# First-level diagonal blocks laid out by ScalarE in free score columns, and fifth-level blocks written without a masked copy, in a two-layer kernel

## The chip, the cores and the metric

The kernel runs on one core of a Trainium2 chip. The metric is the device time in microseconds of one launch; the median of the runs counts. Engines are TensorE (PE in the profile; PEld is its weight load), VectorE (DVE), ScalarE (ACT), GpSimd (POOL) and SyncE (SP), which only issues DMAs here. All run their own instruction streams and meet in semaphores that are written out by hand.

## The reference

Input x is 4 x 1024 x 256 in float32. Two layers follow each other, each an attention-like block and a feed-forward block with modulated layer norms. The change touches one place, the complex linear recurrence of the second layer's first block:

```
c = (silu(x @ W_in.T + b_in) @ W_qkva.T + b_qkva)   # complex q, k, v, a; 8 heads of 32
a = a * (rsqrt(mag2) * sigmoid(log(mag2)))
h_t = a_t * h_(t-1) + k_t (outer) v_t                # associative scan along the sequence
y = einsum('blhd,blhde->blhe', q, h)                 # then W_y, silu, W_out
```

The other parts are a delta-rule attention, a gated mixture of 16 small experts, and a mixture of 8 large experts.

## The kernel before, in words

The sequence is cut into 8 segments of 128 positions, all 4 batches at once. A function `turn` is emitted once per segment on each engine; in it the second part of one segment (`rest`) is interleaved with the delta rule of the next (`nxt`) and the projections of the one after (`pre`). After the segments the large experts run.

In a segment the recurrence is evaluated as masked products of queries and keys, in levels. `HG = 2` groups of `HP = 4` heads alternate. Level k = 0 is the diagonal. Levels k = 1 to 5 (`INNER = 5`) pair neighbours inside blocks of `BLK = 32` positions: at level k the queries of the odd runs of m = 2^(k-1) positions meet the keys of the even runs before them. Levels 6 and 7 join blocks of 32 and of 64. Between two levels VectorE multiplies decay factors into the queries and keys (the loop over `lev` and `hg`, L1454 to L1471 on VectorE; `lev` = k - 1), and TensorE's `level(hg, k)` (L2113) computes the raw scores of level k into PSUM banks 4 hg to 4 hg + 3.

Where the scores go, for one head group:

- `nears[hg]` holds the 32 x 32 diagonal blocks, 4 heads x 4 batches x 2 (real and imaginary) x 32 columns a partition; for group 0 it lies in the tile `h_tok`, for group 1 in `arena`. GpSimd zeroes it and the full score tile `score` earlier in the segment (signal `zeroed`, counts 1 to 6).
- k = 0: VectorE's masked copy at L1362 takes the diagonal from PSUM.
- k = 1: VectorE takes the scores from PSUM by four masked copies, one for each block of 32 partitions (L1370), writing every second column of the near tile. They signal `masked`.
- k = 2 to 5: ScalarE's `take_blocks` (L881) copies the block diagonals from PSUM into `raws[hg]` in four pieces (signal `block_ok`), and VectorE makes one masked copy of 128 partitions from there into the near tile (L1379, signal `masked`).
- Then ScalarE's `lay_near` (L834) lays the near tile into the full scores, `lay_middle` (L845) and `lay_far` (L854) add levels 6 and 7 from PSUM; TensorE's `outputs` (L2128, L2133) follows.

Masks are in `near_masks`. The order on every engine is the order of the code. On VectorE each step of the loop is: the products, a wait for `scored` of the level that still reads the queries, the new queries and keys (signals `q_ready`, `k_ready`), the masked copy of the next level, and a wait for its end. TensorE's `level` waits for the keys, the queries, and for the signal that the former scores have left its banks: `masked` at k = 1 and 2, `block_ok` at k = 3 to 6. ScalarE waits, in front of its first `take_blocks`, for the sixth `q_ready` and the second `k_ready`, since `raws` lies in a table that level 1 reads. SyncE issues the load of the next x behind the first `k_ready`.

Of the kernel before, what the change touches and what calls it, by code (L numbers as in the profile page):

```python
# [24 lines left out]
ACT = mybir.ActivationFunctionType  # L25
AX = mybir.AxisListType

P = 128
B, L, D = 4, 1024, 256
KC = D // P  # L30
SEG = 128
# [91 lines left out]
def build(nc, ins, out):  # L123
    with ExitStack() as ctx:
# [132 lines left out]
        def level_table(hg, lev):  # L257
            n = NT >> lev
            if lev == LEVELS:
# [14 lines left out]
                 for v in (h_tok[:, :, :].rearrange("p b d -> p (b d)"), y2_flat[:, 2 * NT:4 * NT])]  # L274
        Hx, o = carve(o, [P, B, 2, HP, 2 * HD1])
# [85 lines left out]
        masked = signal("masked", rest=12)  # L361
        block_ok = signal("block_ok", rest=8)
# [299 lines left out]
        def _(act):  # L662
# [11 lines left out]
            def turn(seg, rest, nxt, pre):  # L674
                def at(s, k):
                    return s.handle, s.base(seg) + k
# [107 lines left out]
                if rest:  # L784
# [43 lines left out]
                    def lay_near(hg):  # L828

                        act.wait_ge(*at(masked, 2 * INNER + hg + 1))  # L830
                        for pair in range(2):
                            for n in range(NCH):
                                blk = slice(BLK * n, BLK * n + BLK)
                                ins_ = act.activation(score_pairs[hg][pair][blk, :, :, :, blk].rearrange("p h b r t -> p (h b r) t"),  # L834
                                                      nears[hg][blk, 2 * pair:2 * pair + 2].rearrange("p h b r t -> p (h b r) t"),
                                                      ACT.Copy)
                        ins_.then_inc(*up(laid, me))
# [35 lines left out]
                    def take_blocks(k, hg):  # L873
# [5 lines left out]
                        for n in range(NCH):  # L879
                            blk = slice(BLK * n, BLK * n + BLK)  # L880
                            ins_ = act.activation(  # L881
                                raws[hg][blk].rearrange("p (h g t) -> p h g t", h=HP, t=half),
                                banks_[blk, 4 * hg:4 * hg + HP, :].rearrange("p h (g c) -> p h g c", g=2 * B)
                                [:, :, :, half * n:half * n + half], ACT.Copy)
# [4 lines left out]
                    act.wait_ge(*at(q_ready, 3 * HG))  # L889
                    act.wait_ge(*at(k_ready, HG))  # L890
                    for k, hg in itertools.product(range(2, INNER + 1), range(HG)):
                        take_blocks(k, hg)
# [114 lines left out]
        def _(dve):  # L1007
# [69 lines left out]
            def turn(seg, rest, nxt, pre):  # L1077
# [186 lines left out]
                if rest:  # L1264
# [89 lines left out]
                    def take_scores(hg, k):  # L1354
# [12 lines left out]
                        elif k == 1:  # L1367
                            for n in range(NCH):
                                blk = slice(BLK * n, BLK * n + BLK)
                                ins_ = dve.copy_predicated(  # L1370
                                    near_score[blk].rearrange("p h b r (j two) -> p h (b r) j two", two=2)[:, :, :, :, 1],
                                    allow[blk].rearrange("p n m -> p (n m)").unsqueeze(1).unsqueeze(1)
                                    .to_broadcast([BLK, HP, 2 * B, width]),
                                    banks_[blk, 4 * hg:4 * hg + HP, :].rearrange("p h (g c) -> p h g c", g=2 * B)
                                    [:, :, :, width * n:width * n + width])
                            ins_.then_inc(*up(masked, me))
                        else:
                            dve.wait_ge(*at(block_ok, 2 * (k - 2) + hg + 1))
# [55 lines left out]
                    for lev, hg in itertools.product(range(LEVELS), range(HG)):  # L1434
# [37 lines left out]
                        if lev < INNER:  # L1472
                            take_scores(hg, lev + 1)
# [281 lines left out]
        def _(pe):  # L1755
# [32 lines left out]
            def turn(seg, rest, nxt, pre):  # L1788
# [206 lines left out]
                if rest:  # L1995
# [75 lines left out]
                    def level(hg, k):  # L2071
# [7 lines left out]
                        else:  # L2079
                            if lev:  # L2080
                                pe.wait_ge(*at(k_ready, 2 * lev + hg - 1))
                            if lev < 2:
                                pe.wait_ge(*at(masked, 2 * lev + hg + 1))
                            elif lev <= INNER:
                                pe.wait_ge(*at(block_ok, 2 * (lev - 2) + hg + 1))
# [365 lines left out]
```

## Time and profile before

| what | us |
|---|---|
| three runs | 3846.6, 3847.2, 3855.82 |
| median | 3847.2 |
| profiled execution | 3847.57 |
| its span, first to last instruction | 3845.7 |

| engine | busy us | share of the span |
|---|---|---|
| TensorE matmuls | 2886.4 | 75% |
| TensorE weight loads | 2163.0 | 56% |
| VectorE | 2164.3 | 56% |
| ScalarE | 1078.8 | 28% |
| GpSimd | 653.4 | 17% |

The shares are averages over stages with different limits. Of the chain of work that ended last, 57% of the span is TensorE and 21% VectorE. Times in the rows below are counted from the start of the span. The granted clock is given as a share of TensorE's full 2.4 GHz, so 0.50 is its level of 1.2 GHz.

### The profile page before, as it was taken

The page shows a single profiled execution, that of the slowest core. Times are in us where ns is not written, and L with a number is a line of the kernel's source. Part 1 is how long each engine was busy: PE and PEld are TensorE (multiplying, and loading weights), DVE is VectorE, ACT ScalarE, POOL GpSimd, SP SyncE. Part 2 cuts the span into 40 slices and gives each one's busy share as a digit, 9 for nine tenths or more (in the row PEclk, how much of TensorE's full clock was granted, in tenths as well). Part 3 has the DMA queues.
Part 4 walks back from the last instruction along what each step waited for, and adds up shares of the span by engine and source line. Part 5 has one row for each costly group of instructions (what it writes and reads, how often), then busy time and mean ns, then how long its engine had stood idle before and what let it go on. Part 6 is the DMA issues. An engine that isn't in the chain of part 4 may idle for free.

```text
span 3845.7 us, 81835 instructions
## 1 busy us (share of the span) xinstructions
PE 2886.4 (75%) x35776; PEld 2163.0 (56%) x35776; DVE 2164.3 (56%) x4688; ACT 1078.8 (28%) x2076; POOL 653.4 (17%) x682
## 2 busy tenths in 40 slices
PE   4368669867986898499759866986688458999990
PEld 3244457445744664476447545744554447888880
DVE  4445776587659666956685677658544930101004
ACT  0212253124312522333243225312412322222220
POOL 0323300420060016002400420051001000000006
PEclk8577878877787878697868877887779678999995
DMA  2122201210121122012201220121100006565645
GB/s 80 23 56 51 45 2 47 71 29 17 42 71 18 40 46 55 8 40 57 45 7 40 61 45 2 51 67 24 40 23 33 2 21 215 191 193 193 200 152 175
DMA packets 230022, 247.56 MB, mean 64 GB/s; under 512 B 147360, under 2 KB 187168, under 8 KB 227360
## 3 DMA queue, kind: packets, MB, share of 16 engines
q1 hardware_dynamic: 223520, 225.54, 20.6%
q0 software_dynamic: 6144, 16.79, 1.4%
q8 instruction: 282, 4.62, 0.5%
q14 instruction: 76, 0.62, 0.1%
HBM read 196.15 MB, written 46.14 MB: 63 GB/s over the span
## 4 chain that ended last, share of the span: by engine, by line
PE 57%; DVE 21%; ACT 6%; POOL 5%; issue 4%; DMA 1%; SPq 0%; POOLq 0%; DVEq 0%
PE banks L1814 13%; PE banks L2316 7%; PE banks L2335 7%; PE banks L2047 4%; PE banks L2113 3%; POOL arena L1706 3%; PE banks L2128 2%; PE banks L1824 2%; PE banks L2133 2%; PE banks L1941 2%; POOL arena L1750 2%; PE banks L1946 2%; PE banks L1951 1%; PE banks L2069 1%; DVE arena L1468 1%
## 5 line engine op out<-in xcount | busy, mean ns | idle before, releaser
L1706 POOL TENSOR_TENSOR arena<-arena 128x1 f32<-128x1 f32 (+30 forms) x496 | 435.6, 909 | 607.1 <-DMA arena<-n_d 441.0
L2113 PE MATMUL banks<-arena 32*32 32x64 f32 (+2 forms) x6144 | 209.7, 327 | 215.8 <-DVE h_tok L1370 68.2
L1727 POOL DMA_INDIRECT h_d<-h_tok,pos_now x64 | 66.7, 1043 | 1707.4 <-DVE pos_now L1571 1690.3
L1149 DVE TENSOR_REDUCE arena<-arena 128x1 f32<-128x1 f32 (+30 forms) x496 | 243.7, 502 | 172.7 <-POOL arena L1706 168.3
L2113 PE MATMUL banks<-arena,xn 32*32 32x64 f32 (+2 forms) x6144 | 197.6, 330 | 181.7 <-DVE xn L1471 89.1
L2113 PEld LDWEIGHTS banks<-arena 32*32 32x32 f32 (+2 forms) x6144 | 191.4, 202 | 236.7 <-issue 144.8
L1814 PE MATMUL banks<-hT,ring 128*128 128x512 f32 x640 | 313.1, 642 | 8.7 <-DVE arena L1293 8.5
L2113 PEld LDWEIGHTS banks<-arena,xn 32*32 32x32 f32 (+2 forms) x6144 | 181.6, 198 | 196.1 <-issue 98.0
L881 ACT ACTIVATE arena<-banks 32x512 f32<-32x512 f32 x256 | 150.4, 588 | 455.0 <-DVE xn L1471 240.5
L2316 PE MATMUL banks<-arena 128*128 128x256 f32 x1248 | 276.7, 380 | 0.0
L2335 PE MATMUL banks<-arena 128*128 128x256 f32 x1248 | 275.7, 379 | 0.0
L1001 ACT ACTIVATE arena<-banks,arena 128x256 f32<-128x256 f32 x312 | 130.7, 470 | 456.3 <-PE banks L2316 456.3
L2316 PEld LDWEIGHTS banks<-arena 128*128 128x128 f32 x1248 | 238.3, 191 | 32.4 <-issue 0.4
L2335 PEld LDWEIGHTS banks<-arena 128*128 128x128 f32 x1248 | 234.7, 190 | 29.9
L1814 PEld LDWEIGHTS banks<-hT,ring 128*128 128x128 f32 x640 | 126.2, 204 | 187.5 <-issue 187.0
L1814 PE MATMUL banks<-arena,ring 128*128 128x512 f32 x512 | 225.3, 596 | 6.2 <-ACT arena L800 6.2
L2047 PE MATMUL banks<-ring,arena 128*128 128x256 f32 x640 | 159.4, 416 | 27.7 <-DVE arena L1293 27.7
L1651 DVE COPY arena<-banks 128x512 f32<-128x512 f32 x39 | 27.0, 692 | 270.6 <-PE banks L2304 270.6
L1814 PEld LDWEIGHTS banks<-arena,ring 128*128 128x128 f32 x512 | 96.1, 190 | 128.8 <-issue 114.6
L1750 POOL DMA_INDIRECT arena<-y_d,y_at x64 | 64.7, 1011 | 608.7 <-DMA y_d<-arena 589.5
L1661 DVE TENSOR_TENSOR arena<-banks,arena 128x512 f32<-128x512 f32 x39 | 27.0, 692 | 249.4 <-PE banks L2335 249.4
L2047 PEld LDWEIGHTS banks<-ring,arena 128*128 128x128 f32 x640 | 134.7, 212 | 55.8 <-DVE arena L1293 34.3
(337 smaller groups left out, 5247.3 us busy)
## 6 DMA issues: line engine op xcount, KB each, us to landing
arena<-in_w_ring SPq DMA_DIRECT2D x78, 1024.0 KB, 5.0
ring<-in_w_ring SPq DMA_DIRECT2D x104, 512.0 KB, 4.6
arena<-h_d SPq DMA_DIRECT2D x39, 256.0 KB, 5.3
y_d<-arena SPq DMA_DIRECT2D x39, 256.0 KB, 5.8
n_d<-NA SPq DMA_DIRECT2D x8, 1024.0 KB, 3.9
arena<-n_d SPq DMA_DIRECT2D x16, 512.0 KB, 7.5
u_d<-arena SPq DMA_DIRECT2D x8, 1024.0 KB, 3.8
NA<-u_d SPq DMA_DIRECT2D x32, 256.0 KB, 5.6
```

What stands on the lines that cost most here:

```text
L881: ins_ = act.activation(raws[hg][blk].rearrange("p (h g t) -> p h g t", h=HP, t=half), banks_[blk, 4 * hg:4 * hg + HP, :].rearrange("p h ( ...
L1001: ins_ = act.activation(hid1[:, i % 2, t], bank[pair][:, half * T1:(half + 1) * T1], ACT.Gelu, bias=b1[:, i % 2, t:t + 1])
L1149: dve.tensor_reduce(Usub[:, c, 0:t, t], part, AX.X, ALU.add).then_inc(*up(sub_sum, me))
L1706: pool.tensor_tensor(part, Usub[:, c, 0:t, 0:t], Nsub[:, c, t, 0:t].unsqueeze(1).to_broadcast([P, t, t]), ALU.mult)\
L1750: pool.indirect_dma_start(out=y_of[:, s % 3, k, b], out_offset=None, in_=y_d, in_offset=spot)\
L1814: i_ = mm(dst, w[:, k, cols_], rhs(src, k), start=(k == 0), stop=(k == n - 1))
L1824: i_ = mm(bank[banks[j]][:, i * D:(i + 1) * D], src[:, k, 2 * j + i, :], w[:, k, :], start=(k == 0), stop=(k == KC - 1))
L1941: i_ = mm(bank[6 + k][q, j * P:(j + 1) * P], WT[:, k, j, q], S0[:, k, (j - c) % B, :], start=True, stop=True)
L2047: i_ = mm(bank[6 + b // 2][:, (b % 2) * D:(b % 2 + 1) * D], hid0[:, i, b, :], downs[d][:, i - first, :], start=(i == 0), stop=(i == TILES0 ...
L2113: i_ = mm(bank[4 * hg + h][keys, b * width:(b + 1) * width], K2[rows_, r, b, keys], q, start=(r == 0), stop=(r == 1), skip_group_check=True)
L2316: i_ = mm(bank[t // 2][:, (t % 2) * T1:(t % 2 + 1) * T1], w1[:, i % 2, t // 4, at_:at_ + P], h_cols[:, i % 2, k], start=(k == 0), stop=(k ...
L2335: i_ = mm(bank[4 + i % 2][:, j * D:(j + 1) * D], hid1[:, i % 2, t, j * P:(j + 1) * P], w2[:, i % 2, t // 4, t % 4 * D:(t % 4 + 1) * D], st ...
```

## The change

Level 1 takes the path of levels 2 to 4, with a place of its own for the raw blocks: ScalarE copies them from PSUM in four pieces into 16 columns (of the last 32) of the tile `score`, which later lay-outs overwrite, and VectorE makes one masked copy of 128 partitions from there. At level 5 a whole half block (keys 0 to 15, queries 16 to 31 of each block) is wanted and nothing is masked, so ScalarE copies 16 partitions of each block straight into the near tile, and VectorE's masked copy is gone. The waits follow: `masked` has 10 counts a segment in place of 12 and `block_ok` 10 in place of 8.

```diff
+        first_raws = [score[:, :, :, :, SEG - BLK + i * BLK // 2:SEG - BLK + (i + 1) * BLK // 2] for i in range(HG)]
...
                     def lay_near(hg):
 
-                        act.wait_ge(*at(masked, 2 * INNER + hg + 1))
+                        act.wait_ge(*at(block_ok, 2 * (INNER - 1) + hg + 1))
...
                         for n in range(NCH):
                             blk = slice(BLK * n, BLK * n + BLK)
-                            ins_ = act.activation(
-                                raws[hg][blk].rearrange("p (h g t) -> p h g t", h=HP, t=half),
-                                banks_[blk, 4 * hg:4 * hg + HP, :].rearrange("p h (g c) -> p h g c", g=2 * B)
-                                [:, :, :, half * n:half * n + half], ACT.Copy)
+                            made = banks_[blk, 4 * hg:4 * hg + HP, :].rearrange("p h (g c) -> p h g c", g=2 * B)\
+                                [:, :, :, half * n:half * n + half]
+                            if k == 1:
+                                laid_ = first_raws[hg][blk].rearrange("p h b r t -> p h (b r) t")
+                            elif k < INNER:
+                                laid_ = raws[hg][blk].rearrange("p (h g t) -> p h g t", h=HP, t=half)
+                            else:
+                                laid_ = nears[hg][blk].rearrange("p h b r t -> p h (b r) t")[0:half, :, :, half:]
+                                made = made[0:half]
+                            ins_ = act.activation(laid_, made, ACT.Copy)
                         ins_.then_inc(*up(block_ok, me))
...
-                    act.wait_ge(*at(q_ready, 3 * HG))
-                    act.wait_ge(*at(k_ready, HG))
-                    for k, hg in itertools.product(range(2, INNER + 1), range(HG)):
+                    act.wait_ge(*at(zeroed, 4))
+                    for k, hg in itertools.product(range(1, INNER + 1), range(HG)):
+                        if k == 2 and hg == 0:
+                            act.wait_ge(*at(q_ready, 3 * HG))
+                            act.wait_ge(*at(k_ready, HG))
                         take_blocks(k, hg)
...
                         elif k == 1:
-                            for n in range(NCH):
-                                blk = slice(BLK * n, BLK * n + BLK)
-                                ins_ = dve.copy_predicated(
-                                    near_score[blk].rearrange("p h b r (j two) -> p h (b r) j two", two=2)[:, :, :, :, 1],
-                                    allow[blk].rearrange("p n m -> p (n m)").unsqueeze(1).unsqueeze(1)
-                                    .to_broadcast([BLK, HP, 2 * B, width]),
-                                    banks_[blk, 4 * hg:4 * hg + HP, :].rearrange("p h (g c) -> p h g c", g=2 * B)
-                                    [:, :, :, width * n:width * n + width])
-                            ins_.then_inc(*up(masked, me))
+                            dve.wait_ge(*at(block_ok, hg + 1))
+                            dve.copy_predicated(
+                                near_score.rearrange("p h b r (j two) -> p (h b r) j two", two=2)[:, :, :, 1],
+                                allow.rearrange("p n m -> p (n m)").unsqueeze(1).to_broadcast([P, HP * 2 * B, width]),
+                                first_raws[hg].rearrange("p h b r t -> p (h b r) t")).then_inc(*up(masked, me))
                         else:
-                            dve.wait_ge(*at(block_ok, 2 * (k - 2) + hg + 1))
+                            dve.wait_ge(*at(block_ok, 2 * (k - 1) + hg + 1))
...
-                        if lev < INNER:
+                        if lev + 1 < INNER:
                             take_scores(hg, lev + 1)
...
-                            if lev < 2:
-                                pe.wait_ge(*at(masked, 2 * lev + hg + 1))
+                            if lev == 0:
+                                pe.wait_ge(*at(masked, hg + 1))
                             elif lev <= INNER:
-                                pe.wait_ge(*at(block_ok, 2 * (lev - 2) + hg + 1))
+                                pe.wait_ge(*at(block_ok, 2 * (lev - 1) + hg + 1))
```

How it moves instructions on VectorE, at level 1 of head group 0 and the start of the next step (a row has the line, the operation, what it writes and reads, and the signals it waits for). Before:

```order
L1469 TENSOR_SCALAR arena<-arena 128x256 [waits dve_step]
L1470 TENSOR_TENSOR arena<-hT 128x256
L1471 TENSOR_TENSOR arena<-hT 128x256
L1370 COPY_PREDICATED h_tok<-near_masks,banks 32x512 x4
L1454 TENSOR_TENSOR arena<-arena 128x2x256 [waits masked]
```

And after the change, the same place:

```order
L1474 TENSOR_SCALAR arena<-arena 128x256 [waits dve_step]
L1475 TENSOR_TENSOR arena<-hT 128x256
L1476 TENSOR_TENSOR arena<-hT 128x256
L1378 COPY_PREDICATED h_tok<-near_masks,arena 128x512 [waits block_ok]
L1459 TENSOR_TENSOR arena<-arena 128x2x256 [waits masked]
```

Four copies from `banks` (PSUM) have become one from `arena` (where `score` lies), with a wait for ScalarE.

On ScalarE, from the fill of the state tile (L823) to the first groups of `take_blocks`. Before:

```order
L823 ACTIVATE arena<-H 32x4x64 x7
L881 ACTIVATE arena<-banks 32x512 [waits scored,k_ready,q_ready]
L881 ACTIVATE arena<-banks 32x512 x3
L881 ACTIVATE arena<-banks 32x512 [waits scored]
L881 ACTIVATE arena<-banks 32x512 x3
L881 ACTIVATE arena<-banks 32x512 [waits masked,scored]
```

After the change:

```order
L824 ACTIVATE arena<-H 32x4x64 x7
L891 ACTIVATE arena<-banks 32x32x16 [waits scored,zeroed]
L891 ACTIVATE arena<-banks 32x32x16 x3
L891 ACTIVATE arena<-banks 32x32x16 [waits scored]
L891 ACTIVATE arena<-banks 32x32x16 x3
L891 ACTIVATE arena<-banks 32x512 [waits scored,k_ready,q_ready]
L891 ACTIVATE arena<-banks 32x512 x3
```

Two groups of four stand ahead of the former first one, which keeps its waits.

On ScalarE again, from the last groups of `take_blocks` to `lay_near`. After the change (before, the last two groups read `arena<-banks 32x512`, and both L834 rows waited for masked):

```order
L891 ACTIVATE h_tok<-banks 16x32x16 [waits masked,scored]
L891 ACTIVATE h_tok<-banks 16x32x16 x3
L891 ACTIVATE arena<-banks 16x32x16 [waits masked,scored]
L891 ACTIVATE arena<-banks 16x32x16 x3
L835 ACTIVATE arena<-h_tok 32x16x32 [waits block_ok,zeroed]
L835 ACTIVATE arena<-h_tok 32x16x32 x7
L835 ACTIVATE ring<-arena 32x16x32 [waits block_ok]
```

The near lay-out now waits for ScalarE's own signal, no longer for VectorE's.

## Rows read from the trace of the kernel before

**Rows 1.** Chain that ended last, segment 0: start us, us, what.
```profile
482.33 1.31 DVE arena L1370
...
538.39 6.60 PE banks L2113 x128
```

**Rows 2.** Line L1370: durations ns min/median/max; below, who waited (us, times).
```profile
L1370 DVE COPY_PREDICATED h_tok<-near_masks,banks x32: 1266/1282/1293, 467.0 to 3004.9; 32x512 f32<-32x512 int32 x32
...
  PE banks L2113: 129.5, 16
```

**Rows 3.** Timeline of VectorE, segment 0: start us, us, engine, line, what, count.
```profile
451.90 1.28 DVE L1362 COPY_PREDICATED h_tok<-near_masks,banks 128x1024 f32<-128x1024 int32 x1
...
466.99 5.16 DVE L1370 COPY_PREDICATED h_tok<-near_masks,banks 32x512 f32<-32x512 int32 x4
...
472.19 0.69 DVE L1454 TENSOR_TENSOR arena<-arena 128x512 f32<-128x512 f32 x1
...
478.44 5.18 DVE L1370 COPY_PREDICATED arena<-near_masks,banks 32x512 f32<-32x512 int32 x4
...
483.66 0.69 DVE L1454 TENSOR_TENSOR arena<-arena 128x512 f32<-128x512 f32 x1
...
489.00 1.30 DVE L1379 COPY_PREDICATED h_tok<-near_masks,arena 128x512 f32<-128x512 int32 x1
...
490.33 0.69 DVE L1454 TENSOR_TENSOR arena<-arena 128x512 f32<-128x512 f32 x1
```

**Rows 4.** The same timeline, masked copies of level 3 and level 5.
```profile
501.94 0.70 DVE L1379 COPY_PREDICATED h_tok<-near_masks,arena 128x512 f32<-128x512 int32 x1
...
523.95 0.71 DVE L1379 COPY_PREDICATED h_tok<-near_masks,arena 128x512 f32<-128x512 int32 x1
...
524.70 0.69 DVE L1454 TENSOR_TENSOR arena<-arena 128x512 f32<-128x512 f32 x1
```

**Rows 5.** Timeline of GpSimd, TensorE, ScalarE, levels 1 and 2 [idle before <-releaser].
```profile
422.64 3.51 POOL L1716 MEMSET arena<- 128x4096 f32 x1
...
457.64 3.80 PE L2113 MATMUL banks<-arena 32*128 32x128 f32 x64
...
461.22 2.54 PE L2113 MATMUL banks<-arena,xn 32*128 32x128 f32 x64
...
472.26 3.80 PE L2113 MATMUL banks<-arena 32*128 32x128 f32 x64 [8.49 <-DVE h_tok L1370]
...
478.50 2.38 ACT L881 ACTIVATE arena<-banks 32x512 f32<-32x512 f32 x4 [30.25 <-DVE xn L1471]
```

**Rows 6.** Timeline, level 5 of head group 1 onwards: segment 0, then segment 1.
```profile
518.71 2.07 PE L2113 MATMUL banks<-arena,xn 32*128 32x128 f32 x64 [1.68 <-DVE xn L1471]
...
520.84 2.38 ACT L881 ACTIVATE arena<-banks 32x512 f32<-32x512 f32 x4 [1.36 <-PE banks L2113]
...
524.76 5.11 ACT L834 ACTIVATE arena<-h_tok 32x512 f32<-32x512 f32 x8 [1.53 <-DVE h_tok L1379]
...
535.22 3.07 ACT L845 ACTIVATE arena<-banks 32x256 f32<-32x256 f32 x8
...
883.02 3.79 PE L2113 MATMUL banks<-arena,xn 32*128 32x128 f32 x64 [2.81 <-DVE xn L1471]
...
886.88 2.39 ACT L881 ACTIVATE arena<-banks 32x512 f32<-32x512 f32 x4 [4.24 <-PE banks L2113]
...
899.54 3.07 ACT L845 ACTIVATE arena<-banks 32x256 f32<-32x256 f32 x8
```

**Rows 7.** Who waited for line L1379's masked copies: us in total, times.
```profile
  ACT arena L834: 6.1, 4
  ACT ring L834: 0.9, 4
```

**Rows 8.** Stretches of segment 0: us, busy PE, PEld, DVE, ACT, POOL, PEclk, DMA, GB/s.
```profile
536.80:544.00 7.20, 5.61 (x106) 5.64 (x110) 6.99 (x18) 6.30 (x16) 0.00 (x0) 0.50 0.01 2
544.00:551.20 7.20, 7.20 (x89) 5.57 (x84) 6.65 (x22) 2.33 (x7) 0.00 (x0) 0.98 0.00 0
551.20:558.40 7.20, 5.57 (x52) 4.45 (x52) 1.56 (x5) 3.94 (x12) 0.00 (x0) 1.00 0.01 2
```

More of the change, by code:

```diff
@@ L360, in build @@
         q_ready = signal("q_ready", rest=18)
-        masked = signal("masked", rest=12)
-        block_ok = signal("block_ok", rest=8)
+        masked = signal("masked", rest=10)
+        block_ok = signal("block_ok", rest=10)
         state_ok = signal("state_ok", rest=2)
```

## The prediction, made before the changed kernel ran

> **What bounds the kernel now.** The page's busy shares do not say where this edit lands, so I read the chain of work that ended last inside the stretch that the change touches, the score levels of the second layer's first block. In each of the eight segments that stretch is a chain on VectorE: the chain's pieces there are VectorE instructions, among them each of the four narrow masked copies of L1370, then ScalarE's lay-out copies, then TensorE's far levels [rows 1]. VectorE is busy 6.99 of 7.20 us even near the end of the stretch [rows 8]. TensorE only follows: it waited 129.5 us in 16 waits for L1370's copies [rows 2], and in segment 0 it stood 8.49 us before level 2 [rows 5]. So here VectorE's time is worth its full length until its last masked copies; behind those, ScalarE's order decides. The stretch is entered from TensorE's planes and left into TensorE's outputs, and everything behind it (outputs, delta rule, the next segment) is released by its end. I therefore count a gain per segment and multiply by eight. SyncE's next load of x is released by the first k_ready, in front of the first touched copy, and its data are wanted only after level 6, so no queue takes over.
>
> **Part 1, the first level's masked copy (k = 1) on VectorE.** It is now four copies of 32 partitions x 512 elements straight from PSUM, at a median of 1.28 us each [rows 2]. In segment 0 the group for head group 0 starts at 466.99 and the next instruction, L1454, at 472.19, a slot of 5.20 us; for head group 1 it is 478.44 to 483.66, 5.22 us [rows 3]. After the change one copy of 128 partitions x 512 elements reads what ScalarE has laid into the score tile. No row shows this copy, so I bound it. Low: the copies of level 3 and up, the same count from SBUF, 0.70 us [rows 4]. High: level 2's, also the same count from SBUF, 1.30 us, with a slot of 1.33 us from 489.00 to 490.33 [rows 3]. I take the high end. What the slow ones share is the destination: level 1 writes every second element (1.28 us for 512 elements [rows 2]), level 2 writes runs of two (1.30 us), while the identity level, with runs of 32, does 1024 elements from PSUM in 1.28 us [rows 3]. PSUM as a source is therefore not what makes L1370 slow, and the new copy keeps its destination. The saving is 5.20 - 1.33 = 3.87 and 5.22 - 1.33 = 3.89, together 7.76 us a segment. Over eight segments that is **62 us**.
>
> Level 2's copy puts two elements in each run of 8 bytes out of 16 and runs at 1.30 us, where runs of four take 0.70 us [rows 3, 4]. The Trainium skill, "Advanced Engine Details and Errata", section "SBUF Cachelines", says that at least two hits on a 16-byte line are needed to hide the latency; taken as sufficient, writing every second float (also two per line) would run at full speed. By that the copy would take the low end and the sum would grow by 16 x 0.6 = 9.6 us. The trace's level 2, also with two per line, disagrees, so the rule is kept only as a rival below.
>
> **Who feeds that copy.** The change adds a wait on VectorE for block_ok, and behind it are queued the whole of the next level's updates, for which TensorE and ScalarE wait. ScalarE must first lay four pieces. It does such a group in 2.38 us [rows 5]; the new group has the same shape and count and lands in a strided view, as the other lay-out copies do. TensorE ends level 1 for head group 0 at 457.64 + 3.80 = 461.44 and for head group 1 at 461.22 + 2.54 = 463.76 [rows 5]. ScalarE idled 30.25 us before its first group [rows 5], so it would be done at about 463.9 and 466.3. VectorE reaches the first copy at 466.99 and the second at 478.44 - 3.87 = 474.57 [rows 3]. Slack is 3.1 and 8.3 us, so I cost the wait at nothing. The tile must have been zeroed before: GpSimd's memset of the score tile runs from 422.64 to 426.15 [rows 5], 35 us early. The cover ends only if ScalarE's first group ends over 3.1 us later.
>
> **What is late next.** TensorE's level 2 of head group 0 is now released by ScalarE's group and by the keys, which are ready when the masked copy starts (466.99) instead of by its end (472.19), so it starts 5.2 us earlier. ScalarE's level-2 groups, which still wait for the keys of head group 1, start at about 474.6 and, behind TensorE's level 2 of that group (3.8 us), are done by about 477.0 and 480.9. VectorE wants them at 489.00 - 7.76 = 481.24 and some 6.7 us after it. So VectorE stays the bound, with slack of 4 us.
>
> **Part 2, the fifth level without a masked copy.** VectorE loses two copies a segment, from 0.70 to 0.72 us each, with a slot of 0.75 us (523.95 to 524.70) [rows 4]. ScalarE does the same four copies, now on 16 partitions of each block and straight into the near tile; elements per partition stay at 512, so I take 2.38 us again. A group of four on 16 partitions has no row. On VectorE 32 partitions took no less than 128 (1.28 and 1.30 us for 512 elements, [rows 2, 3]), and I take the same of ScalarE; should a part of 16 cost less, the gain below grows by that much. These VectorE copies are on the path only where ScalarE's near lay-out (L834) waits for them. That is 4 segments: 6.1 us for head group 0 and 0.9 us for head group 1 in total [rows 7]. In segment 0 TensorE's last near level ran at the upper clock (2.07 us from 518.71), ScalarE's blocks ended at 523.22 and L834 started only at 524.76, behind VectorE's copy; the middle lay-out started 535.22 - 518.71 = 16.51 us after TensorE's start [rows 6]. In segment 1 the same TensorE level took 3.79 us, ScalarE went on without a gap, and it is 899.54 - 883.02 = 16.52 us [rows 6]. After the change a segment of the first kind needs 16.51 - (6.1 + 0.9) / 4 = 14.8 us; one of the second kind still needs 16.5. With 4 of 8 segments of the first kind the gain is **7 us**; the bounds are 0 (none) and 14 us (all eight). The other VectorE time that part 2 frees is off the path: levels 5 and 6 of VectorE end ahead of the outputs' need, and TensorE's far levels (6.60 us [rows 1]) stand there. A TensorE that idles less between levels may hold its upper level longer; here it fell to 0.50 after the idle of the near levels and rose to 0.98 with the outputs [rows 8]. The Trainium skill, "TensorE: Matmul & The Clock Gate", section "HAM oscillation — how this bites in real kernels", says that idle gaps make the clock fall back; by that the shortened gap would favour the 14 us end. The trace shows both kinds at the same gap, so I do not take it.
>
> **The sum.** 62 + 7 = 69 us. The profiled execution took 3847.57 us (span 3845.7 and 1.9 around it), against a median of 3847.2 of the three runs: 3847.57 - 69 = 3778.6, and on the median **3778 us**, 1.8% faster. About 0.3% (11.5 us) is what a measurement of this kernel can tell from no change.
>
> **Rivals.**
> A. *The wide copy at full rate* (0.70 us in place of 1.30): 3778 - 9.6 = 3768 us. For it: level 3's row with the same count from SBUF. Against it: both sparse destinations at 1.3 us. Chance 0.12.
> B. *Only part 1 reaches the end.* TensorE's last near level falls at the lower clock in all segments, or the clocks of later TensorE-bound stretches shift a little against it: 3847 - 62 = 3785, and to 3795 with some 10 us of such shifts (one of the three runs of before stands 8.6 us above the median). Chance 0.17.
> C. *The freed time becomes a wait.* The wide copy costs double (2.6 us, if both source gaps and destination gaps were paid) or ScalarE's first group ends 1.3 us too late for it in every segment: the gain of part 1 falls to 7.76 - 2.6 = 5.2 us a segment, 41 us, or 3799 us. Against it: L1454, which reads every second element in the first level, takes 0.69 us [rows 3], and there are 3.1 us of slack. Chance 0.05.
> D. *Slower.* One mechanism: the outputs behind the stretch are TensorE-bound and ran at 0.98 and 1.00 of the clock [rows 8]. If the shorter stretch made the clock rise later, each microsecond of TensorE work done at the lower level costs one more. It pays back the 69 us from 8.6 us of such work in each segment; at 11 us it would be 88 us lost, 3847 + 19 = 3866 us. Against it: in segment 0 the clock is up within the slice in which the outputs start, behind the same far levels (busy 5.61 of 7.20 us [rows 8]), and these stay as they are. Chance 0.03.
> That the change does not do what it says can be left out: the order of instructions shows the single wide copy and no copy at level 5. The remaining 0.63 is the forecast, within some 8 us.
>
> **Range.** From A with the full 14 us of part 2 (3761) to B's far end (3795): 3760 to 3795. It leaves out C and D and the edges, under 2 in 10. Faster by over 0.3%: 0.95 (forecast, A, B and C, less 0.02 for a mixture that nearly cancels); within 0.3%: 0.02; slower by over 0.3%: 0.03.
>
> **What would show it.** In the profile after: 16 wide copies at level 1 near 1.3 us and no idle of VectorE before them; L1454's start 1.33 us behind each; 48 masked copies for levels 2 to 4 instead of 64; ScalarE's groups in 2.4 us, two more a segment; TensorE's level 2 no longer waiting for a masked copy; the near lay-out directly behind the blocks in every segment; the way from TensorE's last near level to the middle lay-out 14.8 or 16.5 us by its clock. The period of segments, (3004.9 - 3.9 - 467.0) / 7 = 362 us [rows 2], should shrink by 8 to 9.5 us. I am wrong if VectorE waits for block_ok at level 1, if the copy is far from 1.3 us, or if the TensorE stretches behind run at a lower granted clock.

## The result, and the profile after

| kernel | median us | range | ratio to before, 95% interval |
|---|---|---|---|
| before, same chip | 3846.9 | 3842.8 to 3855.8 | |
| changed | 3784.94 | 3783.5 to 3785.6 | 0.9835 (0.9818 to 0.9853) |

The change saves 62 us, 1.6%. The forecast was 3778 us with a range of 3760 to 3795; the time lies inside, 7 us above the point. The profiled execution took 3784.3 us with a span of 3782.5.

The page's first lines, after the change (busy us, share of the span, instructions):

```profile
span 3782.5 us, 81843 instructions
## 1 busy us (share of the span) xinstructions
PE 2891.0 (76%) x35776; PEld 2168.2 (57%) x35776; DVE 2092.0 (55%) x4624; ACT 1116.4 (30%) x2140; POOL 653.1 (17%) x682
```

VectorE has 64 instructions and 72 us less, ScalarE 64 more and 38 us more. Where VectorE's time sits is seen in the lines of its masked copies (ns min/median/max; first and last start); L1378 is the new wide copy, L1384 those of levels 2 to 4, L835 the near lay-out:

```profile
L1378 DVE COPY_PREDICATED h_tok<-near_masks,arena x8: 1297/1301/1314, 464.5 to 2947.5; 128x512 f32<-128x512 int32 x8
L1378 DVE COPY_PREDICATED arena<-near_masks,arena x8: 1291/1292/1293, 471.9 to 2955.0; 128x512 f32<-128x512 int32 x8
...
L1384 DVE COPY_PREDICATED h_tok<-near_masks,arena x24: 700/710/1301, 478.6 to 2985.7; 128x512 f32<-128x512 int32 x24
```

VectorE's timeline of segment 0 (start us, us, engine, line, what, count), the answer to [rows 3]:

```profile
464.46 1.30 DVE L1378 COPY_PREDICATED h_tok<-near_masks,arena 128x512 f32<-128x512 int32 x1
465.79 0.69 DVE L1459 TENSOR_TENSOR arena<-arena 128x512 f32<-128x512 f32 x1
...
471.93 1.29 DVE L1378 COPY_PREDICATED arena<-near_masks,arena 128x512 f32<-128x512 int32 x1
473.25 0.69 DVE L1459 TENSOR_TENSOR arena<-arena 128x512 f32<-128x512 f32 x1
```

A slot of 5.20 us has become 1.33 us, and neither L1378 row names idle time, so ScalarE's data were there. ScalarE and TensorE at the same place (idle before and releaser in brackets), the answer to [rows 5]:

```profile
459.02 2.39 ACT L891 ACTIVATE arena<-banks 32x512 f32<-32x512 f32 x4 [12.78 <-PE banks L2118]
461.60 2.38 ACT L891 ACTIVATE arena<-banks 32x512 f32<-32x512 f32 x4 [0.19 <-PE banks L2118]
...
464.59 3.80 PE L2118 MATMUL banks<-arena 32*128 32x128 f32 x64 [3.07 <-DVE arena L1476]
```

ScalarE ends its first group at 461.41, 3.05 us before VectorE wants it. TensorE waits 3.07 us for keys before level 2, where it waited 8.49 us for the copies. The fifth level's end, in segment 0 and in segment 7, the answer to [rows 6] (L846 is the middle lay-out):

```profile
508.30 3.67 PE L2118 MATMUL banks<-arena,xn 32*128 32x128 f32 x64 [1.67 <-DVE xn L1476]
...
512.04 2.39 ACT L891 ACTIVATE arena<-banks 16x512 f32<-16x512 f32 x4 [2.97 <-PE banks L2118]
514.46 5.11 ACT L835 ACTIVATE arena<-h_tok 32x512 f32<-32x512 f32 x8
519.58 5.10 ACT L835 ACTIVATE ring<-arena 32x512 f32<-32x512 f32 x8
524.71 3.07 ACT L846 ACTIVATE arena<-banks 32x256 f32<-32x256 f32 x8
```

The same in segment 7:

```profile
2991.35 2.07 PE L2118 MATMUL banks<-arena,xn 32*128 32x128 f32 x64 [1.68 <-DVE xn L1476]
...
3006.14 3.07 ACT L846 ACTIVATE arena<-banks 32x256 f32<-32x256 f32 x8
```

ScalarE runs without a gap from its last blocks on, and waits for VectorE nowhere. But the way from TensorE's level 5 to the middle lay-out is 16.41 us in segment 0 and 14.79 in segment 7: it hangs on TensorE's clock.

Summed over the eight segments from the timelines (segment by segment, start of one instruction to start of another):

| us | before | after | difference |
|---|---|---|---|
| first update of level 1 to first update of level 5 | 467.8 | 404.7 | -63.1 |
| TensorE's level 5 (group 1) to the middle lay-out | 132.1 | 129.2 | -2.9 |
| middle lay-out to the first output | 74.5 | 73.6 | -0.9 |
| whole stretch, first update to first output | 669.6 | 602.7 | -66.8 |
| all else of the span | 3176.1 | 3179.8 | +3.7 |

The first three rows overlap by 0.6 us in each segment, since TensorE starts that level shortly before VectorE's update of level 5; so they add up to 4.8 us more than the whole. Of the rest, the seven gaps between one segment's first output and the next segment's first update grew by 6.3 us (1948.0 to 1954.3), and the time ahead of the first update fell by 2.5 us. So the period of segments shrank from 362.0 to 354.7 us, by 7.3 us, and not by the 8 to 9.5 us that the forecast asked for. Outside the stretch TensorE's gram products (the small products among keys of the delta rule), which no edit touches, took longer. Lines by busy us, mean ns of one | idle us. Before:

```profile
L1910 PE MATMUL banks<-arena 32*32 32x64 f32 x2048 | 57.4, 239 | 12.9 <-issue 12.9
L1906 PE MATMUL banks<-arena 32*32 32x64 f32 x2048 | 56.5, 246 | 19.2 <-issue 14.8 <-ACT arena L772 4.3
```

After:

```profile
L1915 PE MATMUL banks<-arena 32*32 32x64 f32 x2048 | 59.4, 247 | 13.3 <-issue 13.3
L1911 PE MATMUL banks<-arena 32*32 32x64 f32 x2048 | 58.3, 254 | 18.3 <-issue 13.8 <-ACT arena L773 4.3
```

That is 113.9 us before and 117.7 us after, 3.8 us more, as much as all else grew; that the one is the cause of the other is not shown.

### The profile page after: what moved, and what is told of

Same layout as the page of the kernel before. It is cut to its first block, busy times and chain, and to the rows that moved or that the text cites. A ratio compares the mean times of both kernels' runs of the same rounds, so it can differ in the third digit from the quotient of the medians.

```text
span 3782.5 us, 81843 instructions
## 1 busy us (share of the span) xinstructions
PE 2891.0 (76%) x35776; PEld 2168.2 (57%) x35776; DVE 2092.0 (55%) x4624; ACT 1116.4 (30%) x2140; POOL 653.1 (17%) x682
## 4 chain that ended last, share of the span: by engine, by line
PE 59%; DVE 18%; ACT 7%; POOL 4%; issue 4%; DMA 1%; SPq 0%; POOLq 0%; DVEq 0%
PE banks L1819 14%; PE banks L2321 7%; PE banks L2340 7%; PE banks L2052 4%; PE banks L2118 3%; POOL arena L1711 3%; PE banks L2133 2%; PE banks L2138 2%; PE banks L1829 2%; POOL arena L1755 2%; PE banks L1946 2%; PE banks L1951 2%; PE banks L1956 1%; PE banks L2074 1%; PE banks L1925 1%
## 5 line engine op out<-in xcount | busy, mean ns | idle before, releaser
L2118 PE MATMUL banks<-arena,xn 32*32 32x64 f32 (+2 forms) x6144 | 203.1, 335 | 150.0 <-DVE xn L1476 118.7
L891 ACT ACTIVATE arena<-banks 32x512 f32<-32x512 f32 (+1 forms) x288 | 169.2, 588 | 339.3 <-PE banks L2118 270.7
```

What stands on the lines that cost most here:

```text
L891: ins_ = act.activation(laid_, made, ACT.Copy)
L2118: i_ = mm(bank[4 * hg + h][keys, b * width:(b + 1) * width], K2[rows_, r, b, keys], q, start=(r == 0), stop=(r == 1), skip_group_check=True)
```

## The experiments

The runs below were made on other chips, where the kernel before takes 3871, 3872 and 3842 us. So kernels of different groups are compared by their ratio to the kernel before on the same chip, and kernels of one group directly. An interval of a ratio is some 0.0016 to either side, or 6 us. Where an expectation names a time, it means the first chip; carried over to it by the ratio (an estimate), e0 comes to 3788 us, e1 to 3790, e2 to 3845 and e4 to 3777. The groups are e0, e1, e2 and e4; then e3, e5, e6 and e7; then e8 and e9.

**The changed kernel again** (e0). No edit.

> The changed kernel again beside the others on the same chip: 3784 to 3786 us; levels 1 to 4 in 50.6 us a segment. Theory that the clock of TensorE's last near level is set by how the work falls and not by chance: the same segments as in its first trace (all but the last at the lower clock). Rival (chance): about half of the segments at the upper clock, as before.

Measured 3811.97 us, ratio 0.9847 (0.983 to 0.9863). Levels in 50.6 us a segment again. TensorE's level 5 of group 1 took 3.40 to 3.79 us in all eight segments, against 2.07 us in 4 of 8 in the first trace of before and in 5 of 8 in another (e6, below). In both traces of the changed kernel the lower clock prevails there, and so it does in e1, e3, e4 and e7 below, which share the new level 1 and do not fill TensorE's gaps: in whole or in part in 7 or 8 of 8 segments. So it does not look like chance, though the segment that was spared in the first trace (the last) is not spared here.

**The first part alone** (e1).

```diff
-                        act.wait_ge(*at(block_ok, 2 * (INNER - 1) + hg + 1))
+                        act.wait_ge(*at(masked, 2 * INNER + hg + 1))
...
-                        if lev + 1 < INNER:
+                        if lev < INNER:
```

(and level 5 is laid into `raws` again)

> Only the first part of the change: level 1 by ScalarE's lay-out and one wide masked copy; level 5 keeps its masked copy. Theory (the gain is VectorE's path through levels 1 to 5, and the fifth level's copy is almost off it): levels 1 to 4 as short as in the changed kernel, 50.6 us from the first update to the fifth level's, against 58.5 before; the near lay-out waits for VectorE's masked copy only in segments where TensorE's last near level runs at the upper clock; 3785 to 3790 us. Rival (the fifth level's two copies, with slots of 0.75 us in every segment, are on the path): 3785 + 8 x 1.3 = 3795 us or more.

Measured 3815.47 us, ratio 0.9852 (0.9835 to 0.9868), 3.5 us above the changed kernel of the same group. Levels 50.6 us a segment. Who waited for the masked copies of levels 2 to 5, us in total and times:

```profile
  ACT arena L835: 1.5, 1
  ACT ring L835: 0.9, 4
```

Of the fifth level's copies only 2.4 us reach ScalarE in all eight segments, and the stretch is 1.95 us longer in all than with both parts. The 3.5 us between the two medians are within what chance can do, so it is the trace that puts the rival (10 us or more) out: the first part is nearly the whole gain, 55.5 of 59.0 us on this chip.

**The second part alone** (e2).

```diff
+                            if k < INNER:
+                                laid_ = raws[hg][blk].rearrange("p (h g t) -> p h g t", h=HP, t=half)
+                            else:
+                                laid_ = nears[hg][blk].rearrange("p h b r t -> p h (b r) t")[0:half, :, :, half:]
+                                made = made[0:half]
...
-                        if lev < INNER:
+                        if lev + 1 < INNER:
```

(on the kernel before; `masked` and `block_ok` are counted accordingly, and the near lay-out waits for `block_ok`)

> Only the second part: the fifth level laid straight into the near tile and its masked copy gone; level 1 keeps its four narrow copies. Theory: levels 1 to 4 stay at 58.5 us; a segment gains 1.75 us where TensorE's last near level (head group 1) runs at the upper clock, 4 of 8 in the trace of before, nothing elsewhere: 3847 - 7 = 3840 us, from the lay-out starting 14.8 instead of 16.5 us after that level in those segments. Rival (nothing of the second part reaches the end): 3847 us. Rival (two slots of 0.75 us in all segments): 3835 us.

Measured 3869.34 us, ratio 0.9994 (0.9984 to 1.0003). Levels stayed at 58.5 us. The mechanism is there in the trace, in 7 of 8 segments, since in this kernel TensorE's level 5 mostly ran at the upper clock:

```profile
514.78 2.07 PE L2117 MATMUL banks<-arena,xn 32*128 32x128 f32 x64 [1.72 <-DVE xn L1475]
516.91 2.38 ACT L888 ACTIVATE arena<-banks 16x512 f32<-16x512 f32 x4 [1.39 <-PE banks L2117]
519.32 5.10 ACT L834 ACTIVATE arena<-h_tok 32x512 f32<-32x512 f32 x8
...
529.57 3.07 ACT L845 ACTIVATE arena<-banks 32x256 f32<-32x256 f32 x8
```

Level 5 to the middle lay-out is 14.79 us, and the stretch is 13 us shorter in all (656.4 against 669.4 in e6). The time fell by 2 us, inside what can be told from nothing; by the time alone it is the first rival (nothing reaches the end) that was met, and the expected 7 us lies just outside the interval (up to 6 us saved). Between the segments' outputs and the next first update this kernel's trace has 1981.6 us, that of before (e6, on another chip with the same time of before within 1.5 us) 1971.8, seven gaps each. So most of what the stretch gives is taken back outside it, where no instruction was changed.

**A dense destination for the wide copy** (e4). The first level's scores go to 16 neighbouring columns, which are the wrong ones.

```diff
-                                near_score.rearrange("p h b r (j two) -> p (h b r) j two", two=2)[:, :, :, 1],
+                                near_score.rearrange("p h b r (two j) -> p (h b r) two j", two=2)[:, :, 1, :],
```

> The changed kernel, but the wide masked copy of level 1 writes 16 neighbouring columns of each block instead of every second one; so the first level's scores land in wrong columns, and the work is otherwise the same. Theory (a sparse destination sets the 1.30 us): 0.70 us a copy, 16 copies on the path, 3785 - 16 x 0.6 = 3775 us. Rival (the source in strided pieces of 16, or the broadcast mask, sets it): 1.30 us, 3785 us.

Measured 3802.15 us, ratio 0.9818 (0.9801 to 0.9834), 9.8 us under the changed kernel of the same group, and with no run of the one among the times of the other.

```profile
L1378 DVE COPY_PREDICATED h_tok<-near_masks,arena x8: 704/706/717, 463.0 to 2964.9; 128x512 f32<-128x512 int32 x8
L1378 DVE COPY_PREDICATED arena<-near_masks,arena x8: 705/715/717, 469.9 to 2971.8; 128x512 f32<-128x512 int32 x8
```

Source and mask are as in the changed kernel; only the destination is dense, and the copy falls from 1.30 to 0.71 us. 16 x 0.59 = 9.4 us; levels 1 to 4 shortened by 9.3 us in all (404.6 to 395.3), which is the gain within the noise. The sparse destination alone sets the 1.30 us. The Trainium skill, "Advanced Engine Details and Errata", section "SBUF Cachelines", asks for at least two hits on a 16-byte line; read as enough, it does not hold for a masked copy of float32: every second element, two per line, costs 1.30 us, and 16 in a row 0.71 us.

**ScalarE's first groups held back** (e3).

```diff
                     act.wait_ge(*at(zeroed, 4))
+                    act.wait_ge(*at(k_ready, 1))
```

> The changed kernel, but ScalarE's first-level group waits also for the first new keys, which VectorE finishes just before its wide copy. Theory (VectorE's wait costs nothing since ScalarE is 3.1 us early): now the wait is bare, VectorE idles about 2.4 us before the wide copy of head group 0 and nothing before that of group 1; 8 x 2.4 = 19 us slower than the changed kernel, some 0.5%. Rival (VectorE has slack elsewhere that takes the delay up): within 5 us of the changed kernel.

Measured 3830.53 us, ratio 0.9887 (0.9871 to 0.9904), 0.0040 above the changed kernel's, or 15 us. The timeline of segment 0 shows the bare wait:

```profile
467.92 4.80 ACT L891 ACTIVATE arena<-banks 32x512 f32<-32x512 f32 x8 [18.91 <-DVE arena L1477]
470.34 1.30 DVE L1379 COPY_PREDICATED h_tok<-near_masks,arena 128x512 f32<-128x512 int32 x1 [2.50 <-ACT arena L891]
...
477.81 1.29 DVE L1379 COPY_PREDICATED arena<-near_masks,arena 128x512 f32<-128x512 int32 x1
```

VectorE idles 20.0 us before the copies of group 0 in 8 segments, and nothing before group 1. The stretch grew by 21.6 us in all, and some 15 of them show in the time. So in the changed kernel the wait is covered, and without the cover each microsecond of it is paid in the stretch.

**The kernel before, with a profile, on the chip of e3** (e6).

> The kernel before, unchanged, with a profile on the chip that runs the others of this group, to sort the time outside the score levels. Levels 1 to 4 in 58.5 us a segment, the whole stretch from the first update to the outputs 83.3 to 84.1 us. Theory (part of the gain is given back outside the stretch, by TensorE's clock): the time outside the stretch is some 3 to 8 us less in all than in the changed kernel on the same chip. Rival (the outside is the same and only start-up differs): equal within 2 us.

Measured 3874.52 us, 1.0003 (0.9993 to 1.0012) of the other runs of the same kernel on this chip. The stretch is 669.4 us in all, as on the first chip. Its span is 3870.2, so 3200.8 us lie outside; in the changed kernel (e0) it is 3810.0 - 604.0 = 3206.0 us. That is 5.2 us more after the change, beside 3.7 us more on the first chip. But e0 ran on another chip, the changed kernel itself has no run on this one, and two chips differ by as much: all four kernels of e0's group, e2 among them, have 3206.0 to 3209.1 us outside, and of the three others on this chip e3 has 3203.9, e5 3195.2 and e7 3196.1. So the comparison that was expected was not made.

An estimate for one chip at a time is the median less the stretch, against the same for the kernel before (669.4 us of stretch on this chip, 669.6 on the first; 669.5 is taken for the two on which it has no trace). Outside the stretch, in us more than the kernel before on the same chip:

| changed, first chip | e0 | e1 | e2 | e4 | e3 | e7 | e8 | e5 | e9 |
|---|---|---|---|---|---|---|---|---|---|
| +4.9 | +6.5 | +8.1 | +11.5 | +8.6 | +2.0 | +1.0 | +8.6 | -5.0 | -6.2 |

Each is uncertain by the 6 us of its ratio. But all are above zero except e5 and e9, the two runs of the one kernel that has both parts and filled gaps (below). So the direction of the theory is likely; that TensorE's clock is the cause is not shown. Segment 5 of the first chip's traces fits such a cause: 30 us around the next segment's gram products, before the change (columns as in [rows 8]):

```profile
2488.50:2518.50 30.00, 24.76 (x572) 16.97 (x572) 20.83 (x67) 9.16 (x17) 7.60 (x8) 0.92 0.29 86
```

After the change:

```profile
2442.00:2472.00 30.00, 24.86 (x566) 18.26 (x565) 18.93 (x60) 9.08 (x17) 8.08 (x8) 0.74 0.24 80
```

With 0.74 for 0.92 of the clock the gap from this segment's outputs to the next first update was 278.8 instead of 275.5 us.

**TensorE's gaps filled** (e5 and, in a later group, e9). Extra matmuls go into banks that the next level overwrites; the wait for the keys moves behind them.

```diff
+                    FILL = {(2, 0): 2, (2, 1): 3, (3, 0): 2, (3, 1): 2, (4, 0): 2, (4, 1): 2, (5, 0): 2, (5, 1): 2,
+                            (6, 0): 1, (6, 1): 3}
+
+                    def fill(hg, k):
+                        for _ in range(FILL.get((k, hg), 0)):
+                            mm(bank[4 * hg][:, :], ident, w_out[:, :, :].rearrange("p k c -> p (k c)"), start=True, stop=True)
```

> The changed kernel with extra matmuls of 128 columns of weights by 512 into banks that the next level overwrites, 1 to 3 before each of levels 2 to 6, in TensorE's idle time. Nothing of the result hangs on them. Theory (the second part brings little because TensorE's level 5 now runs at the lower clock; with a higher clock its 1.7 us come out): level 5 of head group 1 in 2.07 us, the middle lay-out 14.8 us after it in all 8 segments, 8 x 1.5 = 12 us less in the stretch. Rival (the clock there does not follow TensorE's work, or the extra matmuls delay the levels): no change or a loss of some us.

Measured 3791.84 us, ratio 0.9797 (0.9781 to 0.9813): 0.0050 under the changed kernel's ratio, some 19 us, and 80 us under the kernel before. (On the second group's chip the changed kernel had no run; its ratio is that of e0.)

```profile
502.97 2.07 PE L2126 MATMUL banks<-arena 32*128 32x128 f32 x64 [1.50 <-DVE arena L1476]
504.97 1.98 PE L2081 MATMUL banks<-w_out,consts 128*128 128x512 f32 x4
508.44 2.07 PE L2126 MATMUL banks<-arena,xn 32*128 32x128 f32 x64 [1.49 <-DVE xn L1476]
```

Of the 64 passes of levels 2 to 5 (8 segments, two groups) all but one run at the upper clock (2.07 to 2.10 us where the changed kernel has up to 3.80; one of level 4 takes 3.55), the mean granted clock is 0.857 (0.805 in e0), and the middle lay-out follows level 5 after 14.8 us in all eight segments. The stretch is 593.9 us in all, 10 us under e0; the other 9 us of the 19 lie outside it. The gaps are not closed: 1.49 us of idle is left before level 5 of group 1, where the changed kernel has between 1.67 and 3.41 us. The Trainium skill, "TensorE: Matmul & The Clock Gate", section "HAM oscillation — how this bites in real kernels", says that idle gaps make the clock fall back; with the gaps filled, the trace agrees.

**The filled kernel with and without the second part** (e8 and e9). e8 is e1 with the same extra matmuls.

> Level 1 by ScalarE and the wide copy, level 5 with its masked copy as before the change, and the extra matmuls in TensorE's gaps as in the filled kernel. So it differs from the filled kernel by the second part alone, with TensorE's level 5 at the upper clock in all segments. Theory (the second part is worth 1.75 us a segment where that level is at the upper clock, and nothing where it is at the lower): the middle lay-out starts 16.5 us after level 5 in every segment against 14.8, and the time is 8 x 1.7 = 14 us above the filled kernel. Rival (the second part is worth nothing at any clock, and the filled kernel gained by the clock alone): within 3 us of it.

> The filled kernel again, beside the one with the masked fifth level. Theory: level 5 of head group 1 in 2.07 us and the middle lay-out 14.8 us after it in all segments, 0.980 of the time of before, 14 us under the one with the masked copy. Rival (its first gain was chance): 0.985 of before, as the changed kernel.

Measured 3786.88 us for e8, ratio 0.9852 (0.9836 to 0.9868), and 3760.80 us for e9, ratio 0.9788 (0.9774 to 0.9803). The end of the levels in the timeline of e8:

```profile
510.60 2.07 PE L2123 MATMUL banks<-arena,xn 32*128 32x128 f32 x64 [1.49 <-DVE xn L1473]
...
516.63 5.10 ACT L835 ACTIVATE arena<-h_tok 32x512 f32<-32x512 f32 x8 [1.51 <-DVE h_tok L1381]
521.96 5.10 ACT L835 ACTIVATE ring<-arena 32x512 f32<-32x512 f32 x8 [0.23 <-DVE arena L1381]
527.08 3.08 ACT L846 ACTIVATE arena<-banks 32x256 f32<-32x256 f32 x8
```

In e9:

```profile
509.00 2.07 PE L2126 MATMUL banks<-arena,xn 32*128 32x128 f32 x64 [1.49 <-DVE xn L1476]
...
513.54 5.10 ACT L835 ACTIVATE arena<-h_tok 32x512 f32<-32x512 f32 x8
518.67 5.10 ACT L835 ACTIVATE ring<-arena 32x512 f32<-32x512 f32 x8
523.79 3.07 ACT L846 ACTIVATE arena<-banks 32x256 f32<-32x256 f32 x8
```

With the clock held up, the waits of 1.51 and 0.23 us for the masked copies are there in each segment of e8 and gone in e9: 16.48 against 14.79 us, 13.6 us in all, of which 11.3 reach the first output. The rival (under 3 us) is out. But the two kernels differ by 26 us, nearly twice the 14 that were expected, and 10.8 us of that lies in the seven gaps outside the stretch, where the gram products take 118.7 us in e8 and 112.0 in e9; this time the outside went the other way than in e2. So the 11.3 us of the stretch are what the second part is shown to bring here, and the rest of the 26 us is not explained. And e8, with the first part and the filling but the masked fifth level, has the ratio of e1 without filling (0.9852) and its stretch within 0.5 us (605.4 against 605.9): as far as these show, filling pays only once the masked copy is out of ScalarE's way. e9 has a lower ratio than the changed kernel in either of its groups.

**The near lay-out of group 1 on GpSimd** (e7). ScalarE makes only group 0's; GpSimd copies group 1's behind the last `block_ok`, with a signal of its own for TensorE.

```diff
-                    for hg in range(HG):
-                        lay_near(hg)
+                    lay_near(0)
...
+                    pool.wait_ge(*at(block_ok, 2 * (INNER - 1) + 2))
+                    for pair in range(2):
+                        for n in range(NCH):
+                            blk = slice(BLK * n, BLK * n + BLK)
+                            ins_ = pool.tensor_copy(score_pairs[1][pair][blk, :, :, :, blk].rearrange("p h b r t -> p (h b r) t"),
+                                                    nears[1][blk, 2 * pair:2 * pair + 2].rearrange("p h b r t -> p (h b r) t"))
+                    ins_.then_inc(*up(near1, me))
```

> The changed kernel, but the near lay-out of head group 1 (eight copies, 5.1 us on ScalarE) is made by GpSimd beside ScalarE's lay-out of group 0. Theory (behind level 5 ScalarE's order is the bound, with VectorE some 2 us behind it): the middle lay-out starts 5.1 us earlier, but the outputs then wait for VectorE's level 7 queries, so only 2 us a segment are gained, 16 us or 0.4%. Rival (GpSimd's copies slow VectorE down through their shared way to the memory, or take longer than 8 us): no gain or a loss.

Measured 3815.59 us, ratio 0.986 (0.9844 to 0.9876), no better than the changed kernel's 0.9847: the rival was right. The middle lay-out does start 5 us earlier, but the stretch is 76.5 us in every segment against 75.3 to 75.7 in e0. GpSimd's eight copies in the timeline of segment 0:

```profile
513.12 6.73 POOL L1731 COPY ring<-arena 32x512 f32<-32x512 f32 x8 [68.63 <-ACT arena L892]
```

VectorE's steps in e7 in the 8 us while they run (busy us, mean ns of one | idle us):

```profile
L1473 DVE TENSOR_TENSOR arena<-arena 128x512 f32<-128x512 f32 x2 | 1.7, 838 | 0.1
...
L1475 DVE TENSOR_TENSOR xn<-hT 128x256 f32<-128x256 f32 x1 | 0.9, 854 | 0.0
```

The same steps in the changed kernel, in an equal stretch:

```profile
L1473 DVE TENSOR_TENSOR arena<-arena 128x512 f32<-128x512 f32 x2 | 1.4, 692 | 0.1
...
L1475 DVE TENSOR_TENSOR xn<-hT 128x256 f32<-128x256 f32 x1 | 0.4, 417 | 0.0
```

VectorE's last queries end at 532.78 + 0.29 in segment 0 and the outputs start at 533.18: the bound has passed to VectorE, and beside GpSimd VectorE is slower. It starts its update of level 7 (group 0) 72.4 us after the first update, where the changed kernel does so after 69.5 us; these 2.9 us are more than the 2 us that were to be gained. The Trainium skill, "SBUF — State Buffer", section "Who interferes with whom", says that a VectorE instruction with two SBUF inputs contends with GpSimd reading SBUF; the rows agree, 854 against 417 ns for one.

## Why the prediction was right, and where its sizes were off

- **What bounds the stretch.** Right: levels 1 to 4 shortened by what VectorE lost there.
- **The wide copy.** Taken at 1.30 us from level 2's row and because of the shared sparse destination; measured 1.29 to 1.30, with its cause shown by e4. Part 1 was put at 62 us and measured 63.1: for group 1 the old copies also started 0.11 us later behind L1471 than the new one does, which the slots left out.
- **The wait for ScalarE.** Put at nothing with 3.1 us of slack; 3.05 measured, and e3 shows its price without cover (predicted for e3 19 us, measured about 15, the stretch 21.6).
- **Part 2.** The mechanism was right and the size was off: 7 us from 4 of 8 segments at the upper clock, measured 2.9 us to the middle lay-out and 3.8 to the output. The step that failed was to take the clock's pattern of before over to the changed kernel. In the changed kernel TensorE's level 5 is at the lower clock, in whole or in part, in 7 of 8 segments. The sentence that a shorter gap might hold the clock up and bring 14 us pointed the wrong way; only filled gaps did (e5, e9). Nor do [rows 6] show both kinds at the same gap, as the forecast says: they have 1.68 us before the fast one and 2.81 before the slow one. The trace does have the case elsewhere, in segment 7 (1.68 us before 3.80 us), so the idle just before the level does not by itself decide its clock.
- **All else.** I counted nothing outside the stretch in the forecast; it took 3.7 us. A named sign of being wrong, a lower granted clock in TensorE's work behind the stretch, did come in segment 5 (0.74 for 0.92). Rival B had this and the clock of level 5, and the measured 3785 us is its figure. The profiled execution missed the forecast for it (3778.6 us) by 5.7 us: 3.2 us less from part 2 and 3.7 us lost outside, less the 1.1 us that part 1 brought beyond its term. So the main term put the time inside the range, and the rest went as in rival B, to which the forecast gave a chance of 0.17.
- **Rivals A and C** were decided by rows: 1.30 us, and no idle time before L1378. D did not happen.

Open stays why the outside of the stretch moves by up to 11 us with no instruction of it changed. In two pairs on one chip the gram products move with it: 3.8 us in the first pair, and 6.7 of the 12.0 us between the outsides of e8 and e9. But e3 has 3.1 us more outside than e6 on the same chip and 3.0 us less in its gram products (133.1 against 136.1), and in e6 and e0, on two chips, they take much the same time (136.1 and 135.0 us). The one segment shown has a lower granted clock around them, so the clock is a likely part of the cause and not shown to be all of it. No run changes the clock there alone.

## What to carry to other kernels

A masked copy should be as wide in partitions as the engine allows: four copies on 32 partitions cost four times one on 128, and laying the data out by an idle engine first is free as long as that engine is ready when the busy one asks; work out that slack from both timelines. Before counting a wait away, ask which clock the releasing TensorE work will have afterwards: here the second part took 2 us from the stretch as the kernel stood (e1 against e0), and 11 us with TensorE kept busier (e8 against e9).

## What the runs showed of the hardware

A masked copy of float32 on VectorE takes 1.30 us for 512 elements when its destination is every second element or pairs, and 0.71 us with runs of four or more, from SBUF; from PSUM the sparse destination costs the same (1.28 us), and 1024 elements in runs of 32 take 1.28 us too [rows 3]; ordinary two-input operations with every second element as input (L1459, first level) take 0.69 us. ScalarE's copy of 512 elements a partition takes 0.59 us on 16 partitions as on 32. The kernel before, the same program, took 3847, 3871, 3872 and 3842 us on four chips. In e6 its gram products (L1906, L1910, 2048 matmuls each) took 282 and 279 ns in the mean against 246 and 239 on the first chip; that is 22 us of busy time, of 24.5 us between the two spans. Why is open.
